# A window-attention and dynamic-convolution kernel: the values as three single-pass products

## What is computed

```python
q = to_grid(_conv1x1(x, Wq, bq))      # Wq, Wk, Wv: 128 x 128
k = to_grid(_conv1x1(x, Wk, bk))
v = to_grid(_conv1x1(x, Wv, bv))
attn = jnp.einsum('bgck,bgcl->bgkl', q, k) / np.sqrt(Cs).astype(np.float32)
attn = jax.nn.softmax(attn, axis=-1)
out = jnp.einsum('bgkl,bgcl->bgck', attn, v)
...
x = x + out
h = jax.nn.gelu(_conv1x1(x, W1, b1), approximate=False)
x = x + _conv1x1(h, W2, b2)
```

## Time and profile before

| | |
|---|---|
| median of 3 runs | 5636.39 us (5632.51 to 5637.9) |
| the profiled execution, its own time | 5632.41 us |
| its span | 5630.7 us |
| attention stage, about | the first 1850 us |
| PE / PEld busy | 5481.4 / 3958.4 us |
| DVE / POOL / ACT busy | 5188.5 / 4333.2 / 3475.8 us |

### The profile page before, as it was taken

How to read it: one execution, slowest core, us unless ns; L and a number is a source line. 1 busy time by engine, 2 the same in 40 slices (tenths; PEclk the granted TensorE clock), 3 DMA queues, 4 the chain that set the end, 5 groups by cost and what they waited for, 6 DMA issues and landing times.

```text
span 5630.7 us, 113420 instructions
## 1 busy us (share of the span) xinstructions
PE 5481.4 (97%) x38408; PEld 3958.4 (70%) x38408; DVE 5188.5 (92%) x5447; ACT 3475.8 (62%) x4284; POOL 4333.2 (77%) x1895
## 2 busy tenths in 40 slices
PE   8999999999999599999999999999999999999998
PEld 7888888888887266666666666666666666666666
DVE  7888888888888699999999999999999999999998
ACT  6888888888887355555555555555555555555553
POOL 4555555555555588988888888888888888888885
PEclk9999999999999799999999999999999999999999
DMA  2222222222221222222222222222222222222221
GB/s 90 73 75 73 72 75 72 74 74 74 74 74 60 57 68 76 62 75 65 67 74 68 72 69 73 63 77 63 68 72 68 72 70 72 65 77 61 69 71 44
DMA packets 155247, 394.18 MB, mean 70 GB/s; under 512 B 35136, under 2 KB 38400, under 8 KB 155136
## 3 DMA queue, kind: packets, MB, share of 16 engines
q1 hardware_dynamic: 154800, 392.87, 22.9%
q10 hardware_dynamic: 400, 0.69, 0.1%
HBM read 219.37 MB, written 136.31 MB: 63 GB/s over the span
## 4 chain that ended last, share of the span: by engine, by line
PE 47%; DVE 13%; issue 5%; POOL 1%; SPq 0%; DVEq 0%; ACT 0%; DMA 0%; POOLq 0%; ACTq 0%
PE ps_k L877 18%; PE ps_t L894 15%; DVE products L1106 9%; PE ps_m L860 7%; PE ps_p L846 4%; DVE products L1112 2%; PE ps_t L902 1%; DVE ps_k L1106 1%; PE ps_t L911 1%; PE ps_m L867 1%; POOL enh L811 1%; PE ps_t L909 1%; DVE products L1068 0%; DVE h_prod L1126 0%; SPq L690 0%
## 5 line engine op out<-in xcount | busy, mean ns | idle before, releaser
L811 POOL TENSOR_TENSOR enh<-enh,tap 128x1280 f32<-128x1280 f32 (+1 forms) x1024 | 2515.4, 2456 | 144.0 <-ACT tap L1015 90.5
L1106 DVE TENSOR_TENSOR products<-ps_k,enh 128x1024 f32<-128x1024 f32 x1664 | 1995.3, 1218 | 93.7 <-PE ps_k L877 79.9
L877 PE MATMUL ps_k<-att,basis 128*128 128x512 f32 x4608 | 1695.3, 453 | 60.3 <-DVE products L1112 17.3
L1015 ACT ACTIVATE tap<-e,dw 128x1280 f32<-128x1280 f32 (+1 forms) x1024 | 1249.9, 1252 | 219.1 <-POOL enh L811 219.1
L877 PEld LDWEIGHTS ps_k<-att,basis 128*128 128x128 f32 x4608 | 715.3, 190 | 806.5 <-DVE products L1106 501.2
L302 POOL TENSOR_TENSOR hidden_lo<-hidden,hidden_hi 128x1024 fp32r<-128x1024 f32 x256 | 692.8, 2726 | 717.5 <-DVE hidden_hi L507 717.5
L817 POOL TENSOR_TENSOR products<-products 128x1024 f32<-128x1024 f32 x320 | 766.4, 2395 | 356.1 <-DVE products L1106 356.0
L1106 DVE TENSOR_TENSOR ps_k<-ps_k,enh 128x1024 f32<-128x1024 f32 x640 | 785.9, 1228 | 38.6 <-PE ps_k L877 27.6
L894 PE MATMUL ps_t<-ident_swap,products 128*128 128x128 f32 x5376 | 807.9, 273 | 0.0
L894 PE MATMUL ps_t<-ident,products 128*128 128x128 f32 x5376 | 806.3, 272 | 0.5 <-DVE products L1112 0.5
L1112 DVE TENSOR_TENSOR products<-ps_k,products 128x1024 f32<-128x1024 f32 x640 | 783.2, 1224 | 19.7
(11 more groups left out here) (111 smaller groups left out, 7388.0 us busy)
## 6 DMA issues: line engine op xcount, KB each, us to landing
xin<-layer_out SPq DMA_DIRECT2D x64, 1280.0 KB, 7.4
xt<-in_x SPq DMA_DIRECT2D x128, 512.0 KB, 4.1
layer_out<-xo SPq DMA_DIRECT2D x128, 512.0 KB, 2.9
x_own<-layer_out SPq DMA_DIRECT2D x128, 512.0 KB, 3.9
out<-out_sb SPq DMA_DIRECT2D x256, 256.0 KB, 2.0
att<-att_hi SPq DMA_DIRECT2D x512, 32.0 KB, 1.9
att<-att_lo SPq DMA_DIRECT2D x512, 32.0 KB, 1.9
h_up<-h_sb SPq DMA_DIRECT2D x256, 16.0 KB
```

Source lines behind the costliest of these rows:

```text
L811: nc.gpsimd.tensor_tensor(own, own, tap_sb[add % TAP_BUFFERS][:, 0:hi - lo, :], ALU.add).then_inc(dw_done, 1)
L877: mm = nc.tensor.matmul(ps_k[KERNEL_BUFFER[q]][:, BANK * s:BANK * (s + 1)], basis[:, 2 * t + s, :], att[p][:, j, :], start=True, stop=True)
L1015: nc.scalar.activation(tap_sb[add % TAP_BUFFERS][:, 0:hi - lo, :], src, ACT.Copy, scale=dw[:, t:t + 1]).then_inc(tap_ready, 1)
L1106: nc.vector.tensor_tensor(out, kernels, enh[p][:, r:r + CHUNK_ROWS, dx:dx + W].unsqueeze(1).to_broadcast([C, 2, CHUNK_ROWS, W]), ALU.mult) ...
```

## The change

`values` no longer multiplies xw by wT at full precision. For each pair of windows it issues three single-pass products into the same PSUM columns: x_hi by w_hi, x_hi by w_lo, x_lo by w_hi, all with 128 pixels as the weights and 128 streamed columns. It doesn't wait for xw_ready any more. Since PE now reads x_hi and x_lo until the values are done, `split_input` waits for all six counts of the tile before. `keep_input` no longer waits for the values of the tile whose xw buffer it overwrites.

```diff
-                def values(m, p, h):
-
-                    if h == 0:
-                        pe.wait_ge(xw_ready, m + 1)
+                def values(m, h):
+
                     pe.wait_ge(qkv_ready, 6 * m + 2 + h)
                     for j in range(PAIRS // 2):
-                        mm = nc.tensor.matmul(ring[1 + h][:, C * j:C * (j + 1)], xw[p][:, PAIRS * h + 2 * j:PAIRS * h + 2 * j + 2, :], wT[:, 2, :],
-                                              start=(j == 0), stop=(j == PAIRS // 2 - 1), skip_group_check=True)
+                        out, pair = ring[1 + h][:, C * j:C * (j + 1)], slice(PAIRS * h + 2 * j, PAIRS * h + 2 * j + 2)
+                        nc.tensor.matmul(out, x_hi[:, pair, :], w_hi[:, 2, :], start=(j == 0), stop=False, skip_group_check=True)
+                        nc.tensor.matmul(out, x_hi[:, pair, :], w_lo[:, 2, :], start=False, stop=False, skip_group_check=True)
+                        mm = nc.tensor.matmul(out, x_lo[:, pair, :], w_hi[:, 2, :], start=False, stop=(j == PAIRS // 2 - 1),
+                                              skip_group_check=True)
                     mm.then_inc(qkv_done, 1)
...
                 def split_input(l, p):
 
                     dve.wait_ge(x_in[p], uses(l, p, 16) + 16)
-                    at_least(dve, qkv_done, 6 * l - 2)
+                    at_least(dve, qkv_done, 6 * l)
...
                     dve.wait_ge(x_lo_ready, 2 * l + 2)
                     at_least(dve, x1_ready, 2 * (l - 3))
-                    at_least(dve, qkv_done, 6 * (l - 3))
                     nc.vector.tensor_copy(windows(xw[p][:, :, :]), xt[p % 2][:, :, :].rearrange("c h (w v) -> c w h v", v=GS)).then_inc(xw_ready, 1)
```

More of the change, by code:

```diff
@@ L414, in step @@
                         project(m)
-                        values(m, (s - 1) % TILE_RING, 0)
-                        values(m, (s - 1) % TILE_RING, 1)
+                        values(m, 0)
+                        values(m, 1)
                         window_scores(m)
```

## The result

| | before | after |
|---|---|---|
| median of 5 runs | 5634.74 us (5630.9 to 5637.9) | 5725.33 us (5722.7 to 5726.44) |
| ratio, 95% interval | | 1.0163 (1.0151 to 1.0175) |
| profiled execution's span | 5630.7 us | 5721.0 us |

A forecast was written before the change was run, and what follows sets the result against it. PE was taken as the bound, with the ring of DVE and POOL just behind. +112.6 us for the longer values block less 17 of stalls gave +96, hence 5732 against the median of 5636.4; range 5668 to 5790.

The forecast's parts named there:

- The price of a product: On PE in values: each pair of weight load and product costs 0.11 us in either precision, bounded by 0.056 and 0.232.
- The block: PE's values products up to the score products: pairs go from 16 to 24, +0.88 us a tile, +112.6 us over 128 tiles.
- The stalls that vanish: PE's waits for POOL's hidden_lo in about every third attention step disappear: 0.14 us over some 120 steps, -17 us.
- The later casts: DVE's x_hi casts, released about 1.7 us nearer the scores, cost nothing under PE's 14.86 us step; uncovered, 0.35 a tile.
- the ring: DVE hidden_hi, POOL hidden_lo, DVE x_hi casts, rest of DVE's step: 14.47 us with blocked casts, 0.39 to spare.
- The ring with free casts: The same DVE and POOL cycle when casts don't wait for hidden_lo: row_sum waits for the exponential, and the cycle is short.
- PE held up by the ring (1): Attention steps of some 15.15 us rather than 14.86, 36 us more: 5768, up to 5790; chance 0.12.
- Full-precision speed at narrow width (2): PE's narrow single-pass values products take two pairs each, 0.223 us, block 5.35, +439 us: 6075; chance 0.10.
- a load behind its predecessor's pass (3): PE's values loads don't overlap the pass before: 0.166 us a pair, +263 us: 5900; chance 0.04.
- cheap loads (4, 5): PE's values: (4) repeated x_hi load free, ring binds, 5678, chance 0.07; (5) loads hide at 0.056, casts free, 5560, 0.06.

The follow-up runs named there:

- the two half-size runs: Changed kernel with 64 of 128 columns streamed in each values product: 5724.93 us; changed kernel with 64 columns of weights, all 128 streamed: 5678.58 us.
- the run with both exchanges: Kernel before, with DVE's x_hi casts moved behind the softmax and its xw copy behind add_attention: 5619.03 us, ratio 0.9978.
- the run with the wait alone: Kernel before, with DVE's x_hi casts also waiting for the values of the tile before, nothing added on PE: 5674.31 us, ratio 1.0074.
- the changed kernel with two buffers: Changed kernel with two x_hi buffers used by turns, casts not waiting for the last values, POOL waiting before x_lo: 5729.43 us, ratio 1.0171.
- The runs with two buffers: Two x_hi buffers used by turns, in the changed kernel (5729.43 us, ratio 1.0171) and in the kernel before (5638.52 us, ratio 1.0009).
- the casts alone: Kernel before, with only DVE's x_hi casts moved behind the softmax: 5633.77 us, ratio 0.9999.

## Why the prediction was right

*The price of a product* was the step that mattered, and it held. The forecast took 0.11 us a pair from the load spacing, the transposes and the full-precision pairs; measured was 0.112, and the two half-size runs show that it is the load. Counting passes, with four for true FP32 as the Trainium skill has it (FP8 and Floating Point Precision, TensorE Precision Notes), would have made 16 single-pass products half as dear as eight at full precision; their block came to 1.83 us against 1.88.

*The block* was put at +0.88 us and came to +0.83, or 128 x 0.05 = 6.4 us less in all. Eight pairs at 0.112 would be 0.90; the sum had not foreseen that the second product follows the first after 0.06 instead of 0.11. The first is held back by project's last 512 columns until 1010.09, the second's load starts at that moment too, and its product 0.06 later, as all the following products stand 0.06 behind the start of their loads. The forecast loss was 96 us and the measured one 90.6; the rest of the 7 us between 5732 and 5725 is the kernel before, whose median is now 5634.74 where the forecast started from 5636.4.

*The stalls that vanish* were put at 17 us. The table of waits has none of PE's for hidden_lo after the change. What they were worth is told by the run with both exchanges, which takes them out of the kernel before: 11.9 us between the medians, 14 between the spans (5630.7 and 5616.7). So 17 was some too much, and the block some too dear, and the two errors partly cancel in the total: 106 less 12 to 14 gives 92 to 94, beside 90.6 measured. What the last few us are is not shown.

*The later casts* cost nothing, as forecast, and the price named for a lost cover, 14.47 us a step, was that of the run with the wait alone, to the hundredth. But the ring that PE covers in the changed kernel is not the 14.47 of the prediction. In most turns the first cast meets only the second hidden_lo and the second cast moves behind it (1012.91, 2.61 for both): 14.62, inside the 14.9 that the prediction gave as the most, and 0.18 to spare instead of 0.39. The turns of 15.84, with the probabilities caught by x_lo, it had not foreseen at all. They are longer than PE's step, and no wait of PE follows because the turns between them are shorter and run ahead. That this was enough is in part luck: with the same collision and a hidden_lo longer by 0.7 us, the changed kernel with two buffers had steps of 15.09. The ring with free casts, too, I had described too kindly: I wrote that it is short. The runs with two buffers show that free casts go with a hidden_lo longer by 0.5 us and cost about as much as blocked ones.

*Rivals.* PE held up by the ring (1): not seen, though nearer than the prediction had it. One of its arguments is also misadded: PE comes to its last wait for hidden_lo 924.31 - 920.56 - 0.56 = 3.2 us after the scores start, not 3.4. Full-precision speed at narrow width (2), a load behind its predecessor's pass (3) and cheap loads (4, 5): excluded by starts 0.11 apart. Rival (4) also said why repeated weights might be free: x_hi serves two products in a row, and each still has its load (3072 loads for 3072 products, 0.11 apart).

## What to carry to other kernels

Count weight loads, not passes, when the streamed side is as narrow as the weights: splitting a full-precision product of 128 x 128 into three single-pass ones turned two loads into three and cost nearly half as much again (2.71 us against 1.88), while with 512 columns the load was hidden. Before pricing a later wait, measure the second-longest ring of the step; it tells what the wait costs when its cover goes and what a saving elsewhere can bring at most. A ring's length is not a constant either: it changes with where the operations of two contending engines meet, so take it from several steps, and see whether the short turns make up for the long ones. And when an operation is moved to a place where the other engine is idle, look at what now waits behind it: here the casts alone brought nothing, the casts and the copy together 12 us.

## What the runs showed of the hardware

- DVE's casts and POOL's operations don't run side by side here. A cast that starts without a gap behind hidden_hi runs at once (0.43 us) although POOL's hidden_lo has a start on record before it; so did all 39 such pairs of the kernel before, between 100 and 1750 us. After a gap of 0.16 us or more (77 pairs) the cast waits for the POOL operation to end. The Trainium skill (SBUF — State Buffer, Terms, and Who interferes with whom) has an exclusive lock on a shared port pair, which goes to whoever issues first. The blocked casts agree. So does the longer hidden_lo, as its recorded time contains a wait for DVE. The rows of the kernel before, with blocked and with free casts:

```profile
903.87 0.69 DVE L507 CAST hidden_hi<-hidden 128x1024 fp32r<-128x1024 f32 x1
904.03 2.74 POOL L302 TENSOR_TENSOR hidden_lo<-hidden,hidden_hi 128x1024 fp32r<-128x1024 f32 x1 [5.87 <-DVE hidden_hi L507]
...
918.50 3.41 POOL L302 TENSOR_TENSOR hidden_lo<-hidden,hidden_hi 128x1024 fp32r<-128x1024 f32 x1 [5.87 <-DVE hidden_hi L507]
919.27 0.43 DVE L524 CAST x_hi<-xt 128x512 fp32r<-128x512 f32 x1
```

  DVE's work without a gap ends at 904.56 in the one case and at 919.70 in the other, and hidden_lo ends 2.21 us behind it in both (906.77 and 921.91); it was 2.21 to 2.24 in every step of these two kinds of the kernel before. So DVE, which was running when hidden_lo was issued, held POOL off until its gapless work was done. That casts issued after POOL's operation still go ahead of it, when they follow without a gap, differs from a lock that goes by the order of issue alone. Why a cast that follows a blocked cast without a gap (906.98 in the kernel before) is caught again is not shown.
- The first narrow single-pass product behind a wide one is followed by the next after 0.06 us, and with 64 columns after 0.02 to 0.03. That goes with the columns streamed; from then on the loads hold the products 0.11 apart. Here a product also starts some 0.06 us behind the start of its own load:

```profile
1010.09 0.19 PEld L354 LDWEIGHTS ring<-w_lo,x_hi 128*128 128x128 f32 x1
1010.20 0.19 PEld L355 LDWEIGHTS ring<-w_hi,x_lo 128*128 128x128 f32 x1
```

  (the changed kernel's loads in order of time; their products stand above, at 1010.14 and 1010.26).
